# Router weights of a mixture of experts spread over partitions through memory instead of by selector products

## The reference, cut to what matters

```
t      = layernorm(x)                                    # 10000 x 512
shared = sum over 2 shared experts: gelu(t @ sw1.T + sb1) @ sw2.T + sb2
probs  = softmax(t @ gate_w.T + gate_b)                  # 8 experts
cw     = probs, kept for the two largest of a row, else 0
routed = sum over 8 experts: cw[:, e] * (gelu(t @ rw1[e].T + rb1[e]) @ rw2[e].T + rb2[e])
out    = x + shared + routed                             # each expert has 64 hidden values
```

## Time and profile before

| | |
|---|---|
| median of 3 runs (lowest to highest) | 1699.88 us (1698.68 to 1703.02) |
| the profiled execution: time; span of the trace | 1702.22 us; 1700.5 us |
| mean granted clock of TensorE | 0.981 of full |
| TensorE busy | 1586.2 us, 93% |
| VectorE, ScalarE, GpSimd busy | 54%, 43%, 30% |
| data moved | 271.47 MB, mean 160 GB/s |
| graph layers; mixture of experts | up to about 990 us; the rest |

### The profile page before, as it was taken

The page is one execution under the profiler, slowest core; times in us unless marked ns, Lnnn a source line. Parts: engine busy times, 40 slices in busy tenths (PEclk is TensorE's granted clock), DMA queues, the critical chain, the costliest instruction groups (busy, mean ns, idle before and its releaser), DMA issues. The chain is left out here.

```text
span 1700.5 us, 23999 instructions
## 1 busy us (share of the span) xinstructions
PE 1586.2 (93%) x7903; PEld 1253.3 (74%) x7903; DVE 911.4 (54%) x2179; ACT 725.0 (43%) x1168; POOL 510.6 (30%) x562
## 2 busy tenths in 40 slices
PE   3998999998998999999999818999999999999998
PEld 2676766787786777778888616888888888888887
DVE  3554686877732333335665436555556555655543
ACT  2343444666631222223665514444444444443542
POOL 3682232477732000000467433122112211221100
PEclk9999999999999999999999959999999999999999
DMA  8997999576759999994777650231122112211201
GB/s 243 281 284 227 304 299 284 157 134 123 130 68 276 284 280 280 276 283 162 214 128 131 92 173 0 102 121 75 75 105 119 74 74 109 114 74 74 87 26 44
DMA packets 72773, 271.47 MB, mean 160 GB/s; under 512 B 12550, under 2 KB 12564, under 8 KB 57570
## 3 DMA queue, kind: packets, MB, share of 16 engines
q1 hardware_dynamic: 51922, 223.59, 41.6%
q0 software_dynamic: 20752, 46.65, 15.0%
HBM read 179.82 MB, written 90.34 MB: 159 GB/s over the span
## 5 line engine op out<-in xcount | busy, mean ns | idle before, releaser
L848 POOL TENSOR_TENSOR zr<-zr,xr 128x2048 f32<-128x2048 f32 (+1 forms) x19 | 89.2, 4699 | 395.6 <-DMA xr<-in_x 395.1
L879 ACT ACTIVATE th<-bank 128x512 fp32r<-128x512 f32 x158 | 94.4, 597 | 185.8 <-PE bank L1106 185.5
L1086 PE MATMUL bank<-tth,w1h 128*128 128x512 f32 (+1 forms) x400 | 164.0, 410 | 0.1
L1086 PE MATMUL bank<-ttl,w1h 128*128 128x512 f32 (+1 forms) x400 | 156.5, 391 | 0.0
L1086 PE MATMUL bank<-tth,w1l 128*128 128x512 f32 (+1 forms) x400 | 155.4, 388 | 0.0
L1086 PE MATMUL bank<-w2h,gth 128*128 128x512 f32 x395 | 155.2, 393 | 0.0
L1086 PE MATMUL bank<-w2h,gtl 128*128 128x512 f32 x395 | 154.7, 392 | 0.0
L1086 PE MATMUL bank<-w2l,gth 128*128 128x512 f32 x395 | 154.3, 391 | 0.0
L1362 DVE SCALAR_TENSOR_TENSOR tl<-bank,th 128x512 fp32r<-128x512 f32 x79 | 54.7, 692 | 179.2 <-ACT th L879 179.1
L1086 PE MATMUL bank<-root1h,th 128*128 128x512 f32 x316 | 133.4, 422 | 5.9 <-DVE yout L1384 4.2
L766 POOL DMA_INDIRECT gx<-y,dst_slot x42 | 45.5, 1084 | 297.0 <-ACT xn_e L899 274.4
(11 more groups left out here) (204 smaller groups left out, 3790.0 us busy)
## 6 DMA issues: line engine op xcount, KB each, us to landing
basis_t<-in_gnn_basis SPq DMA_DIRECT2D x64, 896.0 KB
xin<-in_x SPq DMA_DIRECT2D x39, 512.0 KB, 8.7
xin<-y SPq DMA_DIRECT2D x39, 512.0 KB, 6.5
z<-yout SPq DMA_DIRECT2D x39, 512.0 KB, 6.9
xr<-in_x SPq DMA_DIRECT2D x19, 1024.0 KB, 6.8
zr<-z SPq DMA_DIRECT2D x19, 1024.0 KB, 4.8
out<-zr SPq DMA_DIRECT2D x19, 1024.0 KB, 3.9
y<-yout SPq DMA_DIRECT2D x37, 512.0 KB, 9.2
```

What stands on the lines that cost most here:

```text
L848: pool.tensor_tensor(zq, zq, xr[:, q.mod(2), 0:n, :], ALU.add).then_inc(s_zx, 1)
L879: act.activation(th_a[:, s, :], tpb[s][:], f).then_inc(s_hi, 1)
L1086: ins = pe.matmul(out_ap, a(k), b(k), start=first, stop=last)
```

## The change

1. `spread` on TensorE, its matrix `sel` and bank 6's use for it go.
2. ScalarE makes another copy of the turned weights, `cwf` (full precision, first 8 of the partitions). SyncE stores its 8 rows of 512 to memory (`cw_rows`), waits for that, and then loads each expert's row back, repeated over 64 partitions, into `cwb`: eight loads a group. This `spread(q)` is the first thing in SyncE's `group(q)`, ahead of the store of group q - 1 and the loads for group q + 3.
3. VectorE's `weigh` reads `cwb`, in SBUF, where it read bank 6, in PSUM, and waits for the two loads of its column.
4. TensorE turns the weights ahead of the last down pass (j = 3) instead of behind it.
5. The router's first copy into `cw3` goes: the weights are formed there. 13 chained steps stay of 14. `cwt` then has its first ten rows at full weight instead of the high part, and the bias rows for the low part change place with them (`lo_row`).

```diff
--- before.py
+++ after.py
@@ -102,6 +102,8 @@
     records = nc.dram_tensor("records", (P * ET, 2), I32, kind="Internal").ap()
     src_rows = nc.dram_tensor("src_rows", (ET, P), I16, kind="Internal").ap()
     w_dram = [nc.dram_tensor(f"w_dram{l}", (R * ISUB, P, H), F32, kind="Internal").ap() for l in range(2)]
+
+    cw_rows = [nc.dram_tensor(f"cw_rows{i}", (NE, QT * P), F32, kind="Internal").ap() for i in range(2)]
 
     ctx = ExitStack()
     with ctx:
@@ -170,7 +172,6 @@
         gbias = sb("gbias", [P, NE])
         b1 = sb("b1", [P, FC])
         NR2 = NE + 2
-        sel = sb("sel", [P, NE, 64], F32R)
         b2 = sb("b2", [P, H])
         b2lo = sb("b2lo", [P, H])
         b2r = sb("b2r", [P, H], F32R)
@@ -245,9 +246,11 @@
         mx8 = sb("mx8", [P, QT, 8])
         topv = sb("topv", [P, QT, 8])
         rest = sb("rest", [P, QT, NE])
-        cw = sb("cw", [P, QT, NE])
         cwh = sb("cwh", [P, QT, NE], F32R)
         cw3 = sb("cw3", [P, QT, 3, NR2])
+        cw = cw3[:, :, 0, 0:NE]
+        cwf = sb("cwf", [P, QT * P])
+        cwb = sb("cwb", [P, NE // 2, QT * P])
         assert top[0] <= nc.sbuf_usable_end, (top[0], nc.sbuf_usable_end)
 
         bank = [ctx.enter_context(nc.psum_tensor(f"bank{i}", [P, 512], F32)) for i in range(8)]
@@ -336,7 +339,9 @@
         s_qtl = sem("group_lo")
         s_up = sem("up_done")
         s_ge = sem("gelu_done")
-        s_bc = sem("weight_spread")
+        s_cwf = sem("weights_in_rows")
+        s_cws = sem("weight_rows_stored")
+        s_bc = [sem(f"weight_spread{i}") for i in range(NE // 2)]
         s_gs = sem("weighted")
         s_gh = sem("hidden_hi")
         s_gl = sem("hidden_lo")
@@ -647,7 +652,20 @@
                 load_z(Pos(q))
             load_group(Pos(2))
 
+            def spread(q):
+
+                n = tiles_of(q) * P
+                wait(sp, s_cwf, q.times(1, 1))
+                rows = cw_rows[q.mod(2)][:, 0:n]
+                sp.dma_start(rows, cwf[0:NE, 0:n]).then_inc(s_cws, 16)
+                wait(sp, s_cws, q.times(16, 16))
+                for e in range(NE):
+                    half = slice(64 * (e % 2), 64 * (e % 2) + 64)
+                    sp.dma_start(cwb[half, e // 2, 0:n],
+                                 rows[e:e + 1, :].to_broadcast([64, n])).then_inc(s_bc[e // 2], 16)
+
             def group(q):
+                spread(q)
                 if q.i is not None or q.k > 0:
                     store_group(q + (-1))
                 load_group(q + 3)
@@ -687,21 +705,10 @@
             pool.iota(fill_rec[:, :, 0].rearrange("p (u j) -> p u j", j=2), [[0, NPAIR], [P, 2]], base=TRASH,
                       channel_multiplier=1).then_inc(s_pool, 1)
 
-            pool.affine_select(out=lo_row[:], in_=lo_row[:], compare_op=ALU.is_ge, fill=0.0, base=-NR2,
-                               pattern=[[0, 1]], channel_multiplier=1).then_inc(s_pool, 1)
+            pool.affine_select(out=lo_row[:], in_=lo_row[:], compare_op=ALU.is_ge, fill=0.0, base=NR2 - 1,
+                               pattern=[[0, 1]], channel_multiplier=-1).then_inc(s_pool, 1)
+
             pool.wait_ge(s_pool, 15)
-            pool.affine_select(out=lo_row[:], in_=lo_row[:], compare_op=ALU.is_ge, fill=0.0, base=2 * NR2 - 1,
-                               pattern=[[0, 1]], channel_multiplier=-1).then_inc(s_pool, 1)
-
-            picks = b2lo[:, :].rearrange("p (e f) -> p e f", f=64)
-            pool.affine_select(out=picks, in_=picks, compare_op=ALU.not_equal, fill=1.0, base=0,
-                               pattern=[[-1, NE], [0, 64]], channel_multiplier=1).then_inc(s_pool, 1)
-            pool.wait_ge(s_pool, 17)
-            pool.affine_select(out=picks, in_=picks, compare_op=ALU.not_equal, fill=1.0, base=-2 * NR2,
-                               pattern=[[-1, NE], [0, 64]], channel_multiplier=1).then_inc(s_pool, 1)
-            pool.wait_ge(s_pool, 18)
-            pool.tensor_copy(sel[:], picks).then_inc(s_pool, 1)
-            pool.wait_ge(s_pool, 19)
             pool.sem_inc(s_const, 1)
 
             for l in range(2):
@@ -1044,6 +1051,7 @@
             def q_weights(q):
                 n = tiles_of(q) * P
                 wait(act, s_cwt, q.times(1, 1))
+                act.activation(cwf[0:NE, 0:n], bank[7][0:NE, 0:n], ACT.Copy).then_inc(s_cwf, 1)
                 act.activation(cwt[0:3 * NR2, q.mod(2), 0:n], bank[7][0:3 * NR2, 0:n], ACT.Copy).then_inc(s_ct, 1)
 
             def group(q):
@@ -1223,15 +1231,6 @@
                 product(outb[u % 2][:, 0:n], lambda k: w1h[:, k, c * P:(c + 1) * P], lambda k: w1l[:, k, c * P:(c + 1) * P],
                         lambda k: tth[:, s, k, 0:n], lambda k: ttl[:, s, k, 0:n], range(KC)).then_inc(s_up, 1)
 
-            def spread(q, c):
-
-                n = tiles_of(q) * P
-                if c == 1:
-                    wait(pe, s_ct, q.times(1, 1))
-                wait(pe, s_gs, q.times(NE // 2, c - 1))
-                pe.matmul(cnt[:, 0:n], sel[:, 2 * c - 2:2 * c, :].rearrange("p e f -> p (e f)"), cwt[:, q.mod(2), 0:n],
-                          start=True, stop=True).then_inc(s_bc, 1)
-
             def logits(q):
                 wait(pe, s_qtl, q.times(KC, KC))
                 wait(pe, s_ct, q.times(1))
@@ -1258,6 +1257,8 @@
             def down(q, j):
                 wait(pe, s_oe, q.times(QT, j - 3))
                 o = downb[j][:]
+                if j == 0:
+                    wait(pe, s_ct, q.times(1, 1))
 
                 pe.matmul(o, cwt[:, q.mod(2), j * P:(j + 1) * P], b2r[:], start=True, stop=False)
                 for c in range(FC):
@@ -1272,8 +1273,6 @@
                 for c in range(FC):
                     if q.i is not None or q.k or c > 1:
                         up(q, c)
-                    if c:
-                        spread(q, c)
                     if c < KC and not missing(nxt):
                         q_transpose(nxt, c)
                 if not missing(nxt):
@@ -1282,8 +1281,8 @@
                     down(q, j)
                     if j == 0 and not missing(nxt):
                         logits_by_token(nxt)
-                if not missing(nxt):
-                    transpose_weights(nxt)
+                    if j == QT - 2 and not missing(nxt):
+                        transpose_weights(nxt)
 
             for k in range(KC):
                 q_transpose(Pos(0), k)
@@ -1579,8 +1578,8 @@
             def weigh(q, c):
                 n = tiles_of(q) * P
                 wait(dve, s_ge, q.times(FC, c + 1))
-                wait(dve, s_bc, q.times(NE // 2, c))
-                dve.tensor_tensor(gsc[:, (c - 1) % 2, 0:n], gel[:, (5 * q.k + c) % 2, 0:n], cnt[:, 0:n],
+                wait(dve, s_bc[c - 1], q.times(32, 32))
+                dve.tensor_tensor(gsc[:, (c - 1) % 2, 0:n], gel[:, (5 * q.k + c) % 2, 0:n], cwb[:, c - 1, 0:n],
                                   ALU.mult).then_inc(s_gs, 1)
 
             def g_lo(q, c):
@@ -1599,7 +1598,7 @@
                     wait_apart(dve, s_rt, q.times(total, done[0]))
                 return chain, done
 
-            ROUTER = 14
+            ROUTER = 13
 
             def route_a(q, chain):
 
@@ -1630,10 +1629,9 @@
                 for j in range(n):
                     ins = dve.match_replace(rest[:, j, :], topv[:, j, :], pr[:, j, :], 0.0)
                 chain(ins)
+                wait(dve, s_cwt, q.times(1))
                 chain(dve.tensor_tensor(cw[:, 0:n, :], pr[:, 0:n, :], rest[:, 0:n, :], ALU.subtract))
                 chain(dve.tensor_copy(cwh[:, 0:n, :], cw[:, 0:n, :]))
-                wait(dve, s_cwt, q.times(1))
-                chain(dve.tensor_copy(cw3[:, 0:n, 0, 0:NE], cwh[:, 0:n, :].bitcast(F32)))
                 chain(dve.tensor_copy(cw3[:, 0:n, 1, 0:NE], cwh[:, 0:n, :].bitcast(F32)))
                 chain(dve.tensor_tensor(cw3[:, 0:n, 2, 0:NE], cw[:, 0:n, :], cwh[:, 0:n, :].bitcast(F32), ALU.subtract))
                 dve.sem_inc(s_cw3, 1)
```

## The result

| | before | after |
|---|---|---|
| median of 4 runs each (lowest to highest) | 1701.45 us (1698.68 to 1704.48) | 1747.24 us (1735.70 to 1750.99) |
| ratio, 95% interval | | 1.0256 (1.0233 to 1.0279): slower |
| the profiled execution: time; span | 1702.22 us; 1700.5 us | 1748.90 us; 1747.1 us |
| mean granted clock | 0.981 | 0.970 |
| TensorE busy | 1586.2 us, 93% | 1593.3 us, 91% |

The change costs 46 us. The forecast had the sign and the place; its 1717 was 30 us too low, and the time lies 2 us above its range.

A forecast was written before the change was run, and what follows sets the result against it. TensorE, busy throughout the last stage, was taken as the bound. Saved spreads of 17.5 us against 34.4 us of new waits gave +16.9, so 1717 us on the median 1699.88; range 1698 to 1745.

The forecast's parts named there:

- the ring: Transposes, copy, row store, broadcasts, output store, z and x, addition, root, normalisation, exponential, router, next transposes; as predicted 35.3 us.
- The two waits: TensorE waits for `gtl` in the first down pass, 1.85 us, and for router weights at the transposes, 0.5 us more.
- The held `gsc`: VectorE's fourth-column `gsc`, now with two SBUF inputs, is held until 0.55 us after GpSimd's addition ends.
- Rival 1: Full gain: transfers land unseen and GpSimd's addition touches nothing TensorE waits for; -17.5 us, 1682 us; chance 0.12.
- Rivals 2 and 4: Nothing moves, 1699 us, chance 0.10; weights late for their first use at 6.96 us, 1725 to 1745 us, chance 0.10.
- Together E - 17.9 = 2.35 us: TensorE's summed wait in each looped group, E being when GpSimd's addition ends, 20.25 us after the first up product.
- T to X: From the weight transposes on TensorE (T) to the start of GpSimd's addition z + x (X): 19.4 us.
- the bounds: SyncE's issue time per broadcast load, 0.33 to 0.55 us, taken as 0.45; addition start bounded at 13.5 to 17.2 us.
- Root to T: From the start of GpSimd's root through normalisation and router to TensorE's next weight transposes: 11.0 us in looped groups.
- X to E: GpSimd's addition z + x, from its start to its end: 4.85 us.
- E to root: On GpSimd, from the end of the addition to the start of the root chain: 0 us.
- Rival 3: TensorE's clock falls to half after waits of 3.5 us or more: +60 us or so, 1760 us; chance 0.08.

The follow-up runs named there:

- experiments 1 and 2: Changed kernel with the addition z + x on VectorE instead of GpSimd: 1683.23 us; changed kernel with GpSimd's root ahead of its addition: 1689.45 us.
- experiment 3: Kernel before with only the transposes moved ahead of the last down pass: 1714.05 us; changed kernel with them back behind it: 1732.78 us.
- experiment 6: Changed kernel with nine useless TensorE products where it waits in the first down pass of groups 0 to 15: 1738.50 us.
- experiment 4: Kernel before with early transposes, copy, store and broadcasts waited for but unused, spreads kept and `gsc` read from PSUM: 1749.47 us.
- experiment 2: Changed kernel with GpSimd making the root first and the addition behind it: 1689.45 us, ratio 0.9938 to the kernel before.
- e2_memory_only: Changed kernel with the transposes back behind the last down pass; transfers, copy and 13 router steps stay: 1732.78 us, ratio 1.0189 to the kernel before.

## Why the prediction came out so

**Right.** The sign. The mechanism: SyncE's transfers push the output store, with it z and x, GpSimd's addition and all that stands behind it, into a router that the move has left without slack; experiments 1 and 2 take away the addition or the order and the loss is gone, experiment 3 shows each half, and in experiment 6 nine useless products a group don't lengthen the ring. The two waits: in groups 1 to 16, without the first one of each, which is group 0's, 31.2 - 2.4 = 28.8 us in the down pass and 16.3 - 3.8 = 12.5 at the transposes. The held `gsc`, and that the sum does not hang on it (experiment 4): the rule of the Trainium skill (GPSIMD Engine Reference, Key points) on VectorE instructions with two SBUF inputs agrees with the 4.72 us here. The weights in time: no first `gsc` waits. Groups 17 to 19 with the gain alone. Rival 1, the full gain, is what the kernel would do if the root could start earlier, which was named as its condition: experiment 2 does that. Rivals 2 and 4 are refuted by the trace after.

**The step that failed** is the size of the waits, "Together E - 17.9 = 2.35 us" and the sum of 34.4 us made with it. Measured against the unhindered 32.85, the delay in groups 1 to 16 is 587.6 - 525.6 = 62.0 us, 3.9 a group. By TensorE's timeline that is 41.2 us of recorded waits, 3.8 more because each of the 24 waits is counted only from the modelled end of the product before, 0.18 in each of the 16 groups behind the wait (2.9), and 1.55 of half clock in each of nine (14). For half clock the sum had nothing. The 14 are not what the clock costs, since a later TensorE waits less; experiment 6 has that. The mechanism was right and the terms were too small. By the links of the ring, over the 15 groups with a full addition:

- T to X: 19.4 predicted, 20.49 measured, +1.07, 16 us in all. Of this, 0.6 is in every group: eight broadcasts took 5.21 us with their hand-over instead of 3.6 (0.6 each, above both of the bounds, 0.33 and 0.55), while the store of the rows came back in 1.47 instead of 2.1. From the output store to the addition group 10 took 12.2 us, where 11.3 + 1.0 were counted. The rest is in seven groups with T to X of 20.4 to 21.5, where transfers took longer; these runs don't tell why.
- Root to T: 11.0 predicted (10.5 in the unrolled groups, by their 1.85), 11.56 measured, 10 us in all. From root to normalisation took 2.89 us instead of 2.63 (the first step 0.56, not 0.24 as in the earlier trace rows); the hand-over from the last router step to TensorE took 0.2, which I hadn't counted; half clock made 0.4 to 0.7 in five groups and 1.6 in one, some 5 us, which the sum had put at nothing.
- X to E: 4.85 predicted, 4.68 measured, -3 us.
- E to root: nothing predicted, 0.09 in 14 groups and 1.88 in group 13, 3 us.

That is 26 us of the 29.8 by which the profiled execution missed its forecast (1748.9 against 1719.1). The other 3.6 are group 0, counted as 0 (-2 to +2). Of the 62.0, 1.4 is only the base, 32.85 for 32.94, since a spread costs 0.25 us and not 0.23.

On X itself the forecast by the Trainium skill (SBUF — State Buffer, Door 1: The DMA port swizzle), about 16, comes nearer than my 15.4: group 10 has 16.02. But the eight loads follow one another by their issue, 0.6 us each, so this trace neither shows nor refutes its rule, and the nearness may be luck.

**Rival 3.** The clock fell, where the prediction said "A wait near 1.9 us speaks against": in nine of the 16 groups, in six of them after waits of 1.92 to 2.13 us in the first down pass, and in three after some 2.2 us at the transposes. The price that it gave, 60 us, was wrong all the same, since a late TensorE mostly meets weights that are later still. What failed is its condition, 3.5 us or more.

**The bounds.** The load's issue was bounded by two rows and lay above both, and the range was cut off at the forecast's own upper end. A bound from other shapes of transfer ought to have been wider, and a ring without slack passes every error on, once in each of 16 groups.

**What stays open.** Which waits let the clock fall: 2.09, 2.03 and 1.97 us left it at 1.00, 2.12 and 1.92 didn't; of four waits of 2.2 at the transposes one left it; and in `e2_memory_only` so did some of 2.7 to 2.8 us. What the clock costs is known only to within the overlapping intervals of experiment 6. Why transfers took longer in seven groups, which is some 6 us of the 16 in the first link, is not shown either.

## What to carry to other kernels

Ahead of adding transfers to a queue, list what stands behind them on it, follow that through the other engines back to the start of the transfers, and add the links up: if this ring is longer than the busiest engine's period, it is the period, however idle each queue and engine in it looks. A transfer that nobody waits for can still cost by what it delays (1.9% in `e2_memory_only`); here a swap of two calls on GpSimd, or one addition on another engine, turned 2.6% slower into 0.6% and 1.0 to 1.3% faster. A move ahead uses slack that some other chain may need: look for how long the moved step's input had been ready, and undo the move if it buys nothing.

## What the runs showed of the hardware

- Half clock after short waits: TensorE at 0.53 of full right after 2.12 us of waiting, where I had taken 3.5 us as needed. Nine useless products in the place of the wait kept it at 1.00 in all groups but one, and the kernel with more work was no slower (1738.50 against 1747.24 us).
- GpSimd's addition of two SBUF operands doesn't slow VectorE down, it holds it: in every trace here, an instruction with two SBUF inputs that begins meanwhile ends only after the addition does: `gsc` (4.72 for 0.69) and `gtl` (4.99 for 0.69) 0.55 us after it, one of 32 elements a partition (2.13 for 0.19) 0.05 after it. With one input in PSUM it ran in 0.69.
- The same addition took 2.49 us on VectorE in four tiles and 4.6 on GpSimd.
- A 128 KB broadcast of one 2 KB row to 64 partitions holds SyncE's queue for about 0.6 us, against 0.30 for the store of 8 rows.
